# A planner's weights for row maxima, and one broadcast moved down a DMA queue, in an attention kernel

## The chip, the cores and the metric

The kernel runs on one core of a Trainium2 chip. The metric is the device time of one execution in microseconds (us), the median of several. TensorE does the matmuls, VectorE, ScalarE and GpSimd work on tiles beside it, SyncE (SP) issues the DMAs. The profile calls the first four PE, DVE, ACT and POOL; PEld is TensorE's loading of weights.

## What is computed

The input x has 2 batches of 2048 tokens by 512 features, all in fp32. After a layer norm, `xn` goes two ways:

```python
q, k, v = (xn @ W for W in (Wq, Wk, Wv))            # 16 heads of 32
scores  = einsum('bthd,bshd->bhts', q, k) * tril    # masked scores become 0, not -inf
attn    = softmax(scores / 2048**0.5)
s       = einsum('bhts,bshd->bthd', attn, v) @ Wo
g       = silu(layernorm(xn)*gamma+beta @ ternary(weight).T + bias)
out     = x + s * g
```

A masked score is multiplied by zero and so still takes part in the softmax, as exp(0).

## The kernel before, in words

**Three stages.** The first (to about 397 us) makes queries, keys, values and the gate, chunk by chunk of 512 tokens, and stores them to HBM. The second, from about 397 to 1412 us, is attention in 8 *quads*, each of four heads of one batch. The third, the tail, multiplies by Wo in 8 chunks of 512 tokens, 0 to 3 of batch 0 and 4 to 7 of batch 1, multiplies with the gate and adds x.

**Steps of a quad.** A quad has 40 steps (`STEPS`, L31), numbered 0 to 39 here. A step (c, j) takes query chunk c (512 wide) and key tile j (128 rows); the last four steps of each c lie on the diagonal and are 512, 384, 256 and 128 wide. `GROUPS` (L36) takes steps two by two. In a step, for each of the four heads:

- `scores` (L1465) makes the scores two steps *ahead*, one matmul of up to 512 columns, into one of three PSUM banks psS; ScalarE's `exps` (L1053) turns them into weights in Pb.
- `max_scores` (L1359) makes what the planner puts at this step of *row maxima*: scores with queries on the partitions, 512 columns to a PSUM bank psM, of which there are three. VectorE takes the maximum of each bank (L1173 for plain banks, L1170 for banks that end on the diagonal and are masked). TensorE waits for the bank three entries back before it fills it again.
- then comes the step's *section*: `values` (L1488) adds weights times values into psO, all four heads side by side in 8 short matmuls. At steps for which `by_tensor` (L111) holds, 8 more (L1495) add up the weights into psL: the *row sums*. At the other steps GpSimd adds the weights (L914) or, at j = 0, the tile itself is the start of the sum.

`by_tensor` holds in a quad at steps 2, 6, 8, 10, 16, 18, 20, 22, 28, 30, 32, 34, 36, 38 (in the last quad at more). At j = 0 of a chunk, `row_sums` (L1504) follows the section with four times two matmuls from GpSimd's sums, so that section is as long as one with row sums.

**The order on TensorE** is written out in `quad` (L1519 to L1540): the scores and maxima of step s (`ahead(s)`), then the section of s; on a diagonal `ahead(s)`, `ahead(s + 1)`, then both sections.

**The planner.** A quad has 140 banks of maxima (`max_banks`), sorted by the query chunk that they belong to, and four *turns* (transposes of finished maxima, L1349). The maxima of a chunk of queries must be there before its first scores. `UPFRONT` banks of a quad are made in steps 19 to 39 of the quad before, the rest in its own steps 0 to 18; quad 0 makes 102 of its own there. `step_room` (L135) gives each step a weight: the time of its scores, and a `section` term. `max_entries` (L189) goes along (step, head) and hands out the next entries while the cost given out so far is behind the weight passed so far. The result is the *share* of each step and head (`SHARES`), read by TensorE, ScalarE and VectorE alike.

**The tail's DMAs** are all issued by SP in one order (`chunk`, L818). For chunk n: for n < 4, wait for `al_done` of chunk n and request the numerators `ac` of chunk n + 4 (L752); wait for the chunk's outputs (L828) and store them (L829); for n < 4 request x and gate of chunk n + 4 (`xr`, `gr`, L755, L756). Each is 1 MB. The sums of the softmax of batch 1 are inverted on VectorE (L1241). `spread(1)` (L740), at n = 1, waits for them, puts them to HBM (L743, 32 KB), waits until they have landed (L744), waits for the last products of batch 0 (L745) and issues 16 requests that read them back, each broadcast over 32 partitions (L748, `rb`). Only chunk 7 needs `rb`: GpSimd multiplies its numerators by it (L958). For each other chunk of batch 1 the numerators come already divided.

For chunk n ScalarE makes `ah` (L1061) from `ac`, VectorE `al`, the rest of it (L1258), then TensorE 32 matmuls with `ah` (L1565) and 16 with `al` (L1555); VectorE multiplies by the gate (L1295, `sg`) and adds x (L1297, `oo`), each in four pieces. VectorE makes `al` of chunk n + 1 before the outputs of chunk n. Outputs of chunk n wait for the store of chunk n - 2 to land.

Of the kernel before, what the change touches and what calls it, by code (L numbers as in the profile page):

```python
# [13 lines left out]
P = 128  # L14
B, T, D, H = 2, 2048, 512, 16
# [5 lines left out]
CW = 512  # L21
# [62 lines left out]
def width(s):  # L84
    c, j = STEPS[s]
    return CW - max(0, j - CT * c) * P
# [15 lines left out]
def by_gpsimd(s, last):  # L102


    c, j = STEPS[s]
    if last and c > 0 and (on_diagonal(s) or (c, j) in [(3, 7), (3, 11)]):
        return False
    return j % 2 == 1 or not last and (c, j) in EXTRA


def by_tensor(s, last):  # L111
    return STEPS[s][1] > 0 and not by_gpsimd(s, last)
# [22 lines left out]
def step_room(s):  # L135


    c, j = STEPS[s]
    ahead = STEPS[(s + 2) % NSTEP]
    scores = 1.1 + 4.4 * (CW - max(0, ahead[1] - CT * ahead[0]) * P) / CW  # L140
    section = 1.5 * width(s) / CW
    return scores / 2.5 + section - (1 if j == 0 else 0)


# [28 lines left out]
NX = 4  # L173
# [93 lines left out]
def build(nc, x, Wq, Wk, Wv, Wo, Wf, bias, gamma, beta, out):  # L267
    top = ExitStack()
    with top:
        def sem(name):  # L270
            return top.enter_context(nc.semaphore(name))

        def sbuf(stack, name, shape, dt):
            return stack.enter_context(nc.sbuf_tensor(name, shape, dt))
# [17 lines left out]
        r_rows = nc.dram_tensor("r_rows", [B * H, CW], F32).ap()  # L292
# [67 lines left out]
        lr = sbuf(pc, "lr", [P, H * CW // P], F32)  # L360
# [118 lines left out]
        lrec_done = sem("lrec_done")  # L479
        r_out = sem("r_out")  # L480
# [59 lines left out]
        def numerators(b, c):  # L540
            return num_t[bass.ds(b * D, D), c * CW:(c + 1) * CW].rearrange("(k p) w -> p k w", p=P)
# [43 lines left out]
        def _(sp):  # L585
# [116 lines left out]
            def store_last(qn):  # L702

                c, cols = NCH - 1, slice((NCH - 1) * CW, NCH * CW)
                sp.wait_ge(ost_done, START + qn * NCH + c + 1).then_inc(sp_waited, 1)
                sp.dma_start(num_t[bass.ds(qn * P, P), cols], cum[c % 2][:]).then_inc(ost_out[c % 2], 16)
                sp.wait_ge(lst_done, START + qn * NCH + c + 1).then_inc(sp_waited, 1)
                sp.dma_start(l_rows[bass.ds(qn * HQ, HQ), :], E[c % 2][::DH, :]).then_inc(lst_out, 16)

            def divisors(qn, c):  # L710


                i = c % 2
                sp.wait_ge(lst_done, START + qn * NCH + c + 1).then_inc(sp_waited, 1)
                for h in range(HQ):
                    sp.dma_start(lc[h * DH:(h + 1) * DH, :], E[i][h * DH:h * DH + 1, :]).then_inc(lc_in, 16)  # L716
# [20 lines left out]
            def denominators(b):  # L737
                sp.dma_start(lr[:], l_rows[bass.ds(b * H, H), :].rearrange("r (a w) -> (r a) w", w=H * CW // P)).then_inc(lr_in, 16)

            def spread(b):  # L740

                sp.wait_ge(lrec_done, b + 1)
                sp.dma_start(r_rows[bass.ds(b * H, H), :].rearrange("r (a w) -> (r a) w", w=H * CW // P), lr[:]).then_inc(r_out, 16)  # L743
                sp.wait_ge(r_out, (b + 1) * 16)  # L744
                sp.wait_ge(mul_done, START + b * KT)  # L745
                for k in range(KT):
                    for h in range(HQ):
                        sp.dma_start(rb[h * DH:(h + 1) * DH, k, :],  # L748
                                     r_rows[bass.ds(b * H + k * HQ + h, 1), :].broadcast_to([DH, CW])).then_inc(r_in, 16)

            def load_numerators(b, c):
                sp.dma_start(ac[c][:], numerators(b, c)).then_inc(ac_in[c], 16)  # L752
# [5 lines left out]
            def quad(qn, par, more, follows):  # L758
                if follows:
                    store_last(qn - 1)  # L760
                    load_chunk(qn, 1)
                    sp.wait_ge(pv_done, START + qn * NSTEP)
                if not more:

                    sp.wait_ge(lst_out, START + NQ * 16)
                    denominators(0)
                    sp.dma_start(wo_s[:], w_o).then_inc(wo_in, 16)

                if follows:
                    store_maxima(qn, 2)  # L770
                divisors(qn, 0)
                back(qn, 0)
                if not follows:
                    store_maxima(qn, 2)
                store_divided(qn, 0)
                load_chunk(qn, 2)
                if more:

                    load_half(qn + 1, 1 - par, 1)
                else:  # L780
                    for i in range(2):
                        sp.wait_ge(ost_out[i], START + NQ * NCH // 2 * 16)
                    load_numerators(0, 0)
                    load_numerators(0, 1)
                divisors(qn, 1)
                store_maxima(qn, 3)
                back(qn, 1)
                if more:
                    load_values(qn + 1, 1 - par)
                    store_maxima(qn + 1, 0)  # L790
                else:
                    load_numerators(0, 2)
                    sp.wait_ge(pv_done, START + qn * NSTEP + STEPS.index((2, 0)))
                    load_xg(0)
                divisors(qn, 2)
                store_divided(qn, 1)
                load_chunk(qn, 3)
                back(qn, 2)
                store_divided(qn, 2)
                if more:  # L800
                    load_chunk(qn + 1, 0)
                    store_maxima(qn + 1, 1)
                else:
                    spread(0)
                    sp.wait_ge(wo_done, 2)
                    load_numerators(0, NDIV)
                if qn + 2 < NQUAD:

                    sp.wait_ge(pv_done, START + qn * NSTEP + STEPS.index((NCH - 1, NT // 2)))
                    load_half(qn + 2, par, 0)  # L810
            quads(quad)
            store_last(NQUAD - 1)
            attention_over(sp)
# [3 lines left out]

            def chunk(n, b, c):  # L818
                if n == 1:
                    spread(1)  # L820
                if n + NX < NCHUNK:

                    sp.wait_ge(al_done, START + (n + 1) * KT)
                    load_numerators(1, c)

                parts = [slice(j, j + 1) for j in range(CT)] if n + 1 == NCHUNK else [slice(0, CT)]
                for part in parts:
                    sp.wait_ge(oo_done, START + n * CT + part.stop)  # L828
                    sp.dma_start(out_v[n][:, part], oo[c % 2][:, part]).then_inc(oo_out[c % 2], 16)  # L829
                if n + NX < NCHUNK:  # L830
                    load_xg(n + NX)
# [767 lines left out]
```

## Time and profile before

| | |
|---|---|
| three timed runs | 1515.99 us median (1511.0 to 1517.45) |
| the profiled execution | 1510.48 us, its span 1508.8 us |
| granted TensorE clock, mean | 0.995 |
| busy: TensorE / VectorE / ScalarE / GpSimd | 1474.0 / 1045.3 / 772.3 / 922.6 us |
| HBM | 201 MB moved, 133 GB/s mean |

The span is the time from the first to the last instruction of the program; the profiled execution's own time is 1.7 us longer. In a timeline a row gives start, duration, engine, line, operation, and how many like it were merged; in square brackets stands the idle time before it and who ended it. TensorE's matmuls overlap, so their pace is read from the distance of their starts.

### The profile page before, as it was taken

Reading aid. Unit: us, or ns where it says so; the run is one execution under the profiler, and the core shown is the slowest. Engines: PE = TensorE matmul, PEld = TensorE weight load, DVE = VectorE, ACT = ScalarE, POOL = GpSimd, SP = SyncE. Lnnn points to the kernel's source line nnn. Section 1 sums busy time; section 2 is a strip of 40 time slices with the busy share of each in tenths; the row PEclk is TensorE's granted clock in tenths of the full one; section 3 lists DMA queues with packets and bytes.
Section 4 is the critical chain, followed back from the end, with each engine's and each line's share of the span. In section 5 each row is a group of like instructions: output and inputs, shape, how many; then the busy total and the mean of one; then the engine's idle time right before and its main releaser. Section 6 shows DMA issues by size and latency. Waiting matters only on the chain.

```text
span 1508.8 us, 24424 instructions
## 1 busy us (share of the span) xinstructions
PE 1474.0 (98%) x8458; PEld 898.5 (60%) x8458; DVE 1045.3 (69%) x2413; ACT 772.3 (51%) x1615; POOL 922.6 (61%) x747
## 2 busy tenths in 40 slices
PE   6999999999999999999999999999999999999998
PEld 5888888888544455555555545555554554554686
DVE  7546566554688777777777777777777777773557
ACT  4333223332455666666566665666665666657311
POOL 4100000000477989888998998989998898867401
PEclk9999999999999999999999999999999999999999
DMA  6668965557834425242451533525145152123687
GB/s 206 183 179 235 264 182 170 159 161 202 229 86 109 104 54 113 84 108 54 104 127 30 136 88 74 112 68 122 44 109 134 30 112 81 51 85 128 229 291 297
DMA packets 118395, 201.25 MB, mean 133 GB/s; under 512 B 23264, under 2 KB 40800, under 8 KB 117248
## 3 DMA queue, kind: packets, MB, share of 16 engines
q1 hardware_dynamic: 118272, 199.69, 48.2%
q8 instruction: 67, 1.10, 0.3%
q14 instruction: 56, 0.46, 0.1%
HBM read 123.02 MB, written 76.09 MB: 132 GB/s over the span
## 4 chain that ended last, share of the span: by engine, by line
PE 83%; DVE 8%; DMA 4%; SPq 2%; ACT 2%; issue 1%; POOL 0%; ACTq 0%; DVEq 0%; POOLq 0%
PE psP L1384 21%; PE psS L1465 17%; PE psO L1488 17%; PE psM L1359 16%; PE psL L1495 6%; DVE mx L1173 3%; DVE psM L1170 2%; PE psT L1309 2%; PE psL L1504 2%; DMA out<-oo 1%; ACT acc L1053 1%; PE psD L1565 1%; DMA lc<-E 1%; SPq L716 1%; DMA r_rows<-lr 1%
## 5 line engine op out<-in xcount | busy, mean ns | idle before, releaser
L1053 ACT ACTIVATE Pb<-psS 128x512 f32<-128x512 f32 (+3 forms) x1215 | 563.6, 539 | 361.2 <-PE psS L1465 356.9
L1173 DVE TENSOR_REDUCE mx<-psM 128x1 f32<-128x512 f32 x768 | 484.7, 683 | 136.1 <-PE psM L1359 134.7
L914 POOL TENSOR_TENSOR acc<-acc,Pb 128x1024 f32<-128x1024 f32 (+2 forms) x284 | 543.5, 1943 | 39.9 <-ACT Pb L1053 31.8
L1465 PE MATMUL psS<-half 97*128 97x512 f32 (+1 forms) x1247 | 473.9, 397 | 2.1 <-ACT Pb L1053 0.9
L1359 PE MATMUL psM<-half 96*128 96x512 f32 (+3 forms) x1280 | 458.8, 384 | 10.8 <-DVE mx L1173 4.4
L1465 PEld LDWEIGHTS psS<-half 97*128 97x128 f32 x1247 | 234.8, 190 | 239.4 <-ACT Pb L1053 104.1
L1488 PE MATMUL psO<-Pb,Vs 128*32 128x512 f32 (+3 forms) x2496 | 290.5, 537 | 0.0
L1359 PEld LDWEIGHTS psM<-half 96*128 96x128 f32 x1280 | 236.2, 191 | 83.1 <-DVE mx L1173 32.9
L1170 DVE CUSTOM_DVE_ANT_0 psM<-psM,negm 128x256 f32<-128x256 f32 (+3 forms) x512 | 238.3, 518 | 59.0 <-PE psM L1359 58.5
L914 POOL TENSOR_TENSOR acc<-Pb 128x1024 f32<-128x1024 f32 x48 | 113.4, 2382 | 25.9 <-ACT Pb L1053 25.8
L1190 DVE TENSOR_TENSOR st_lo<-psP,st_hi 128x512 fp32r<-128x512 f32 x64 | 43.9, 688 | 118.0 <-ACT st_hi L1008 118.0
L892 POOL TENSOR_SCALAR_AFFINE_SELECT Pb<-Pb 128x256 f32<-128x256 f32 x240 | 94.0, 407 | 50.9 <-ACT Pb L1053 47.8
L1488 PEld LDWEIGHTS psO<-Pb,Vs 128*32 128x32 f32 x2496 | 56.0, 109 | 94.5 <-issue 44.4
L1495 PE MATMUL psL<-Pb,ones 128*32 128x512 f32 (+3 forms) x976 | 110.9, 526 | 0.0
L852 POOL TENSOR_TENSOR rstd<-ve,mhalf 128x4 f32<-128x4 f32 x8 | 8.1, 1009 | 160.9 <-DVE ve L1106 160.8
L1008 ACT CAST st_hi<-psP 128x512 fp32r<-128x512 f32 x64 | 37.2, 587 | 107.5 <-PE psP L1384 107.4
L1384 PE MATMUL psP<-xh,w_hi 128*128 128x512 f32 x256 | 73.4, 409 | 0.8 <-ACT xh L971 0.8
L1170 DVE DVE_READ_ACCUMULATOR2_ANT mx<- 128x1 f32 x512 | 72.4, 141 | 0.0
L852 POOL TENSOR_TENSOR r<-ve,mhalf 128x4 f32<-128x4 f32 x8 | 8.1, 1009 | 103.7 <-DVE ve L1120 103.7
L1384 PE MATMUL psP<-xl,w_hi 128*128 128x512 f32 x256 | 70.9, 399 | 0.0
L1384 PE MATMUL psP<-xh,w_lo 128*128 128x512 f32 x256 | 70.0, 395 | 0.0
L1495 PEld LDWEIGHTS psL<-Pb,ones 128*32 128x32 f32 x976 | 31.7, 110 | 56.8 <-issue 51.4
(104 smaller groups left out, 1466.3 us busy)
## 6 DMA issues: line engine op xcount, KB each, us to landing
half<-q_hi SPq DMA_DIRECT2D x32, 512.0 KB, 10.0
half<-k_hi SPq DMA_DIRECT2D x32, 512.0 KB, 10.1
q_hi<-st_hi SPq DMA_DIRECT2D x32, 256.0 KB, 4.5
q_lo<-st_lo SPq DMA_DIRECT2D x32, 256.0 KB, 4.9
gate<-gs SPq DMA_DIRECT2D x32, 256.0 KB, 2.2
k_hi<-st_hi SPq DMA_DIRECT2D x32, 256.0 KB, 2.8
k_lo<-st_lo SPq DMA_DIRECT2D x32, 256.0 KB, 3.0
v_quad<-vs SPq DMA_DIRECT2D x32, 256.0 KB, 3.3
```

Of the source, the lines that this page charges most:

```text
L892: g.affine_select(out=tile, in_=tile, compare_op=ALU.is_ge, fill=0.0, base=0, pattern=[[0, 2], [1, P]], channel_multiplier=-1).then_inc(se ...
L914: g.tensor_tensor(to[:, :, o:], one, Pb[s % RING][:, heads, o:], ALU.add).then_inc(sum_done, 1)
L1008: a.copy(st_hi[k % 4][:], psP[k % 4][:]).then_inc(hi_done, 1)
L1053: a.activation(weights(s, h)[:, o:], score_bank(s * HQ + h, last)[:, o:], ACT.Exp, scale=SCALE).then_inc(exp_done, 1)
L1170: ins = v.tensor_tensor_reduce(out=part, in0=part, in1=negm[:, CW - w:], scale=1.0, scalar=-3e38, op0=ALU.add, op1=ALU.max, accum_out=flat ...
L1173: ins = v.tensor_reduce(flat[:, heads, slots], bank[:, 0:ns * w].rearrange("p (a b c) -> p a b c", a=nh, c=w), AX.X, ALU.max)
L1190: v.tensor_tensor(st_lo[k % 4][:], psP[k % 4][:], st_hi[k % 4][:].bitcast(F32), ALU.subtract).then_inc(lo_done, 1)
L1359: ins = t.matmul(bank[:, z * w:(z + 1) * w], Q[tile // HALF][0:STACK, h, tile % HALF * P:(tile % HALF + 1) * P], K[half][0:STACK, h, k0 - ...
L1384: ins = t.matmul(psP[bank][:], left(k), right(k), start=(a + k == 0), stop=(a == len(parts) - 1 and k == KT - 1))
L1465: t.matmul(score_bank(n, last)[:, o:], Ks[par][j // HALF][0:MROW + 1, h, j % HALF * P:(j % HALF + 1) * P], Qs[par][c // 2][0:MROW + 1, h, ...
L1488: ins = t.matmul(psO[hc, o:], V[:, j, hc], weights(s, h)[:, o:], start=(j == 0), stop=(s == last_step[c]), skip_group_check=True)
L1495: ins = t.matmul(psL[h * DH:(h + 1) * DH, o:], ones[:, 0:DH], weights(s, h)[:, o:], start=first, stop=False, skip_group_check=True)
```

## The change

It has two parts. The weight of a step's section in the planner is no longer 1.5 for every step, but 2 where the step takes row sums on TensorE and 1 elsewhere, times the step's width. The entries and their order stay the same; where they are made changes, and `UPFRONT` goes from 75 to 76. The number of entries (banks and turns) at steps 0 to 39, worked out from the code:

```text
quad 0 before  3 4 6 5 5 7 6 7 5 3 5 5 4 7 6 6 6 6 7 4 | 3 3 4 3 3 5 4 4 4 5 4 5 4 4 4 4 3 3 3 2
quad 0 after   3 3 6 5 5 6 9 6 6 3 6 4 4 5 6 5 8 5 8 4 | 3 3 4 4 2 4 4 4 4 5 5 4 5 4 5 3 4 2 4 2
quads 1-6 bef. 2 3 3 4 3 4 4 3 4 2 3 3 3 4 4 4 4 4 5 4 | 3 3 4 3 3 5 4 4 4 5 4 5 4 4 4 4 3 3 3 2
quads 1-6 aft. 2 2 4 3 3 3 5 3 4 2 4 3 2 4 4 3 5 3 6 4 | 3 3 4 4 2 4 4 4 4 5 5 4 5 4 5 3 4 2 4 2
```

Share 30 holds a turn among its entries before and after. In share 18 of quads 1 to 6 all banks lie on the diagonal: one of two 256-wide pieces and four of 384 before, two and four after; the bank that is added comes out of share 17.

The second part takes the put of the reciprocals and the broadcast apart. For batch 1 the put stays at n = 1 and no longer waits for its landing there; the wait and the 16 requests come at n = 3, behind the request for chunk 7's numerators. For batch 0 both stay where they were, one behind the other.

```diff
@@ step_room
-    section = 1.5 * width(s) / CW
+    section = (2 if by_tensor(s, False) else 1) * width(s) / CW
     return scores / 2.5 + section - (1 if j == 0 else 0)
@@ sync engine
-            def spread(b):
-
+            def put_reciprocals(b):
                 sp.wait_ge(lrec_done, b + 1)
                 sp.dma_start(r_rows[bass.ds(b * H, H), :].rearrange("r (a w) -> (r a) w", w=H * CW // P), lr[:]).then_inc(r_out, 16)
+
+            def spread(b):
+
                 sp.wait_ge(r_out, (b + 1) * 16)
                 sp.wait_ge(mul_done, START + b * KT)
@@ quad
                 else:
+                    put_reciprocals(0)
                     spread(0)
@@ chunk
                 if n == 1:
-                    spread(1)
+                    put_reciprocals(1)
                 if n + NX < NCHUNK:
 
                     sp.wait_ge(al_done, START + (n + 1) * KT)
                     load_numerators(1, c)
+                if n == NX - 1:
+
+                    spread(1)
```

## Rows read from the trace of the kernel before

**Rows 1.** The page: busy us (share of the span) and instructions of each engine.
```profile
PE 1474.0 (98%) x8458; PEld 898.5 (60%) x8458; DVE 1045.3 (69%) x2413; ACT 772.3 (51%) x1615; POOL 922.6 (61%) x747
```
**Rows 2.** Stretches: length, busy PE, PEld, DVE, ACT, POOL, clock, DMA share, GB/s.
```profile
409.20:475.11 65.91, 63.11 (x331) 30.71 (x330) 54.70 (x133) 33.42 (x66) 44.49 (x34) 0.97 0.53 109
796.40:923.00 126.60, 125.47 (x792) 65.42 (x791) 96.61 (x246) 78.36 (x172) 113.38 (x92) 1.00 0.38 91
```
**Rows 3.** Waits for VectorE in those two stretches: us, times, longest.
```profile
PEld psM L1359 <- DVE mx L1173: 12.5, 38, 0.4
...
PEld psM L1359 <- DVE mx L1173: 2.8, 8, 0.9
```
**Rows 4.** TensorE's timeline, quad 3: steps 13 to 14, 17 to 18, 24 to 25, 32 to 33.
```profile
834.00 1.07 PE L1488 MATMUL psO<-Pb,Vs 128*32 128x512 f32 x8
...
835.34 0.40 PE L1359 MATMUL psM<-half 96*128 96x512 f32 x1
...
836.75 0.40 PE L1359 MATMUL psM<-half 96*128 96x512 f32 x1
837.08 1.06 PE L1488 MATMUL psO<-Pb,Vs 128*32 128x512 f32 x8
...
847.36 1.07 PE L1488 MATMUL psO<-Pb,Vs 128*32 128x512 f32 x8
850.95 1.07 PE L1488 MATMUL psO<-Pb,Vs 128*32 128x512 f32 x8
...
868.53 1.07 PE L1488 MATMUL psO<-Pb,Vs 128*32 128x512 f32 x8
...
872.93 0.64 PE L1488 MATMUL psO<-Pb,Vs 128*32 128x512 f32 x4
...
897.92 1.06 PE L1488 MATMUL psO<-Pb,Vs 128*32 128x512 f32 x8
...
901.85 1.07 PE L1488 MATMUL psO<-Pb,Vs 128*32 128x512 f32 x8
```
**Rows 5.** Quad 0, sections 15 and 16 on TensorE, and VectorE's six banks between them.
```profile
456.66 1.07 PE L1488 MATMUL psO<-Pb,Vs 128*32 128x512 f32 x8
...
460.80 1.06 PE L1488 MATMUL psO<-Pb,Vs 128*32 128x512 f32 x8
...
458.44 3.68 DVE L1173 TENSOR_REDUCE mx<-psM 128x1 f32<-128x512 f32 x6 [0.45 <-PE psM L1359]
```
**Rows 6.** SP's timeline in the tail.
```profile
1434.62 1.13 SPq L743 DMA_DIRECT2D r_rows<-lr  x1
1446.46 7.49 SPq L748 DMA_DIRECT2D rb<-r_rows  x16
...
1471.58 2.47 SPq L829 DMA_DIRECT2D out<-oo  x1
```
**Rows 7.** Two stretches of the tail, columns as in rows 2.
```profile
1443.00:1456.00 13.00, 13.00 (x59) 10.78 (x58) 7.05 (x12) 2.19 (x4) 0.00 (x0) 1.00 0.44 125
1456.00:1490.00 34.00, 34.00 (x152) 28.09 (x150) 19.97 (x31) 6.86 (x12) 5.48 (x4) 1.00 1.04 386
```
**Rows 8.** Timelines of TensorE, VectorE and GpSimd in the tail.
```profile
1412.03 0.50 PE L1565 MATMUL psD<-wo_h,ah 128*128 128x512 f32 x1
...
1488.32 0.39 PE L1565 MATMUL psD<-wo_h,ah 128*128 128x512 f32 x1
...
1493.84 1.86 PE L1555 MATMUL psD<-wo_h,al 128*128 128x512 f32 x4 [3.55 <-DVE al L1258]
...
1503.75 1.07 PE L1555 MATMUL psD<-wo_h,al 128*128 128x512 f32 x4
...
1485.27 0.69 DVE L1295 TENSOR_TENSOR sg<-psD,gr 128x512 f32<-128x512 f32 x1 [2.72 <-issue]
...
1491.30 2.49 DVE L1258 TENSOR_TENSOR al<-ac,ah 128x512 fp32r<-128x512 f32 x4
...
1482.69 5.48 POOL L958 TENSOR_TENSOR ac<-ac,rb 128x512 f32<-128x512 f32 x4 [69.24 <-DMA ac<-num_t]
```

## Prediction, made before the change was built

> **What bounds the kernel now.** I read the page first. TensorE is busy for 1474.0 us, 98% of the span [rows 1]. A busy TensorE is not yet one at its pace, so I next read stretches: in one middle quad (q3) TensorE is busy 125.47 of 126.60 us and VectorE 96.61, while in the first half of quad 0 VectorE has 54.70 us of work in 65.91 us [rows 2]. The waits say what that means. In that half quad 0 TensorE's weight loads for maxima wait 12.5 us in 38 places for VectorE's plain maxima, in the whole of quad 3 only 2.8 us in 8 [rows 3]. So the middle quads run at TensorE's own pace with a few waits, and the start of quad 0 at VectorE's.
>
> The timeline of single steps gives the two paces. I call an interval the time from one step's section (its psO run, and the psL run where it takes row sums) to the next step's. It holds that section, and then four scores and the *next* step's share of maxima. With four banks an interval takes 837.08 - 834.00 = 3.08 us after a section without row sums and 901.85 - 897.92 = 3.93 us after one with them [rows 4]. Scores and banks alternate there, (836.75 - 835.34)/6 = 0.235 us apart [rows 4]. That is TensorE's price of one more bank. VectorE takes 3.68/6 = 0.61 us for a bank, and with six banks the interval grew to 460.80 - 456.66 = 4.14 us [rows 5].
>
> The tail (from 1412.03) is TensorE's too, 10.88 us a chunk, until 1488.32. Chunk 7 then starts, but its first low-part product comes at 1493.84, after an idle 3.55 us, released by VectorE's al [rows 8]. The way back in the timelines: VectorE makes al for chunk 7 only at 1491.30, behind chunk 5's outputs, which began late, at 1485.27, after an idle 2.72 us [rows 8]. They waited for chunk 3's store, which SP issued at 1471.58, 13.7 us before [rows 6, 8]. SP itself was late: it put the reciprocals at 1434.62 and stood until they had landed, 11.8 us later at 1446.46, then issued 16 spreading requests (7.49 us), so the request for chunk 5's numerators went out only after 1453.95 [rows 6]. Between 1443 and 1456 the DMA engines were at 0.44 of their time, against 1.04 behind it [rows 7].
>
> **Part 1, the shares of maxima.** No instruction is added or removed; the same entries run in the same order. From the code (the diff section has the counts), 11 of some 143 entries of a middle quad change step: shares of steps with row sums grow, the others shrink. TensorE's own work of a quad is conserved, so only waits can change.
>
> What matters is the order in the code: share s stands *ahead* of section s. A larger share at a row-sum step therefore mostly follows a section *without* row sums (steps alternate), and the long section comes only after it. The three psM banks tie them: the last bank of a share of k is issued only when VectorE has done k-3. From [rows 5]: VectorE starts 458.44 - 456.66 = 1.78 us after the section's start, needs 0.61 a bank, and the rest up to the next section is 4.14 - 1.78 - 3 x 0.61 = 0.53. So the interval cannot be shorter than 1.78 + 0.61(k-3) + 0.53: 2.92 for four banks (TensorE's 3.08 decides), 3.53 for five, against TensorE's 3.08 + 0.235 = 3.32. **Five banks after a short section cost a wait of 0.2 us.** After a long section both are 0.85 longer: five banks took 872.93 - 868.53 = 4.40 us, against 3.93 + 0.235 = 4.17, again 0.23 of wait [rows 4].
>
> Middle quad, by interval: shares 6, 16, 32 and 34 go from four banks to five after a short section: +0.8. Share 30 goes to five entries, one a turn: +0.2, taken as the others. Share 18 goes from five entries of small diagonal banks to six; its interval is 850.95 - 847.36 = 3.59 us now [rows 4], and its bound rises to about 4.2 by one more bank of two 256-wide pieces (0.77 us of VectorE), of which 0.24 is TensorE's own: +0.4, less 0.15 in the interval before it, which loses that bank. Shares 25 and 31 go from five to four after a long section: -0.23 each. Sum: 0.8 + 0.2 + 0.25 - 0.46 = +0.8; I take +0.6, since a wait taken in one interval can save one in the next. Six quads: +3.6. Quad 7 has only its own half: +0.6. Quad 0's first half is at VectorE's pace nearly throughout, and there each bank costs 0.61 in whichever interval it stands: 0, between -3 (eight moved entries, each saving 0.61 - 0.235 = 0.37) and +2. Its second half: +0.2. Together **+4.4 us**, bounds -5 (quad 0's -3 and 0.3 in each other quad, a tenth of the 2.8 us of [rows 3]) and +11 (0.3 a moved bank in every quad).
>
> The row gives VectorE 0.61 us from one maximum's start to the next [rows 5]. The Trainium skill ("VectorE: DVE Perf Modes", the section on the TRN2 errata) prices a 512-wide read of PSUM at 120 + 512 cycles of 0.96 GHz, 0.66 us; by that a share of five after a short section would cost 0.1 us more, one taken away after a long section would save 0.1 more, and this part would come to about +7. No sum here uses it; the measured rate is the faster one.
>
> **Part 2, the reciprocals.** `put_reciprocals(1)` stays at chunk 1, the 16 requests move behind the request for chunk 7's numerators. SP goes on at 1434.62 + 1.13 = 1435.8 instead of 1453.95 [rows 6]. It then meets only the full queues: with 1 MB per request at 386 GB/s [rows 7], a request is served every 2.7 us. In order: ac5, out1, xr5, gr5, ac6, out2, xr6, gr6, ac7 (served by 1467), 16 spreads (7.49 us of issuing, about 3 of transfer), out3 served by 1473, xr7, gr7, out4 by 1481. Every DMA that the move passes is counted here: out3 now stands behind the 16 spreads, and still lands some 10 us before the 1485.27 at which VectorE had it. The put has 11.8 us to land and is asked for some 24 us later: no wait.
>
> Against these stand the dates that TensorE sets at 10.88 a chunk. Chunk 5's outputs on VectorE can start when its first product is ready, about 1474.7, and out3 lands at about that time; they end at 1480.1, al for chunk 7 at 1482.6, with 5.7 us to spare, its ah (GpSimd's products 5.48 us after the spreads land near 1471, then ScalarE) by 1480. TensorE reaches chunk 7 at 1488.32 as before and does not stop: it ends at 1488.32 + 10.88 = 1499.2, against 1503.75 + 1.07 = 1504.8 [rows 8]. That takes in the slower matmuls after the idle time, 0.43 apart at 1495.50 and 0.23 at 1488.32 [rows 8]. **-5.6 us.** Bounds: 0 if another wait takes the place, -6 (nothing beyond TensorE's pace is to be had).
>
> **Sum.** 4.4 - 5.6 = -1.2 us against the profiled execution's 1510.48 us (span 1508.8), so 1509.3. That execution is below all three timed runs (median 1515.99, 1511.0 to 1517.45), so for the median: **1514.8 us**.
>
> **Rivals.** *The maxima find room.* If VectorE's backlog, not the next section, is what an interval pays for, each moved entry saves 0.37 wherever VectorE sets the pace: 8 in quad 0 and, in each of 6.6 quads, 3 (17, 25, 31), without the new waits: 28 x 0.37 = -10.4, with the tail -16: 1500. For it: the 12.5 us of waits in quad 0 [rows 3]. Against it: the order in the code, by which the long section comes after the larger share. Chance 0.13.
>
> *VectorE becomes the pace of the middle quads (the other side).* It decides if VectorE is still busy when a share of five begins, because a diagonal bank with its read-out or a row reduction of psO and psL stands in front; then the full 4.14 - 3.08 = 1.06 for two banks is paid, 0.53 for one, and the share of six at step 18 brings the row maxima of the fourth chunk late as well. Then each of the six larger shares costs 0.4 more: 2.4 + 0.6 = 3.0 a quad, over 6.6 quads +20, less the tail's 5.6: 1530. It decides from 2.0 us a quad on, where the sum leaves what can be told from none. For it: 18 is already the worst stretch. Against it: 30 us of VectorE idle in a middle quad [rows 2]. Chance 0.08.
>
> *The tail gains nothing*, if DMA engines at 1.04 with 386 GB/s are the limit [rows 7] and the empty stretch was slack: +4.4, 1520. Against it: the empty 13 us are followed by a wait that TensorE pays. Chance 0.05. That the plan doesn't move anything is ruled out by working the shares out from the code.
>
> **How the numbers follow.** Forecast 0.74, rivals as above. A difference under about 0.5% (7.6 us) can't be told from none. Faster by more takes the first rival and a rest, 0.14; slower the second and a rest, 0.09; same 0.77. Range: the bounds -5 to +11 and -6 to 0 put the sum between -11 and +11; cut at one in ten on each side and with the runs' own spread, 1505 to 1522.
>
> **What would show it.** Right: the intervals that hold shares 6, 16, 32 and 34 at 3.5 us instead of 3.08; those with 25 and 31 at 3.9 instead of 4.40; a middle quad of 127.2 instead of 126.6 us; r_rows at 1435 and no SP gap behind it; DMA share near 1.0 from 1443 to 1456; TensorE without idle time in the tail and no slow matmuls at its end. Wrong: a middle quad under 126 or over 129, a half quad 0 under 63, or VectorE still waiting for a store at chunk 5.

## The result and the profile after

| | before | changed |
|---|---|---|
| median of 20 executions | 1512.9 us (1507.97 to 1519.61) | 1518.03 us (1516.55 to 1521.53) |
| the profiled execution, its span | 1510.48, 1508.8 us | 1517.22, 1515.5 us |
| middle quad 3 | 126.6 us | 127.9 us |
| the tail, from its first product (1412.03, 1424.2) to VectorE's last output | 94.2 us | 88.8 us |

The ratio is 1.003, 95% interval 1.002 to 1.0039: the changed kernel is 5.1 us slower, where the sum had said 1.2 us faster. 1518.03 us lies in the stated range and the difference is within 0.5%, but the sign of the sum was wrong. The forecast of 1514.8 us also started from a median of three runs, 1515.99 us, that was 3.1 us above the one of twenty.

The page of the changed kernel, busy time of each engine, against [rows 1]:

```profile
PE 1479.3 (98%) x8458; PEld 891.5 (59%) x8458; DVE 1045.1 (69%) x2413; ACT 779.5 (51%) x1615; POOL 922.8 (61%) x747
```

The counts are the same and VectorE's work is too. The page alone says nothing more, so I went to the same stretches as before. TensorE's and VectorE's lines stand 6 further down in the changed kernel (L1173 is L1179 there). The changed kernel's quad 3 and three stretches of its tail, columns as in [rows 2]:

```profile
798.80:926.60 127.80, 126.33 (x789) 64.86 (x788) 96.55 (x244) 79.28 (x173) 113.41 (x92) 1.00 0.38 90
1427.00:1455.00 28.00, 28.00 (x126) 23.17 (x125) 18.16 (x29) 4.37 (x8) 0.18 (x1) 1.00 0.98 355
1455.00:1468.00 13.00, 13.00 (x59) 10.78 (x58) 9.72 (x16) 2.19 (x4) 0.00 (x0) 1.00 1.05 398
1468.00:1500.00 32.00, 32.00 (x143) 26.51 (x142) 22.40 (x34) 6.86 (x12) 5.49 (x4) 1.00 0.97 342
```

A middle quad is 1.3 us longer at a granted clock of 1.00 (1.26 to 1.32 in quads 1 to 4 and 6), and VectorE's busy time in it is unchanged. In the tail TensorE now never stops, and the DMA engines have lost their empty stretch (0.44 in [rows 7], 0.98 to 1.05 now).

**Where the quad's time went.** The waits of the changed kernel's quad 3 for VectorE:

```profile
PEld psM L1365 <- DVE mx L1179: 6.2, 18, 0.8
PEld psM L1365 <- DVE mx L1176: 3.2, 9, 0.5
```

[rows 3] had 2.8 us in 8 places for the plain maxima, and the masked ones were at:

```profile
PEld psM L1359 <- DVE mx L1170: 2.5, 8, 0.5
```

TensorE's timeline gives the places (sections 5 and 6, 15 and 16, 17 and 18, 21 and 22, 24 and 25):

```profile
812.38 1.06 PE L1494 MATMUL psO<-Pb,Vs 128*32 128x512 f32 x8
815.98 1.06 PE L1494 MATMUL psO<-Pb,Vs 128*32 128x512 f32 x8
...
842.70 1.06 PE L1494 MATMUL psO<-Pb,Vs 128*32 128x512 f32 x8
846.24 1.06 PE L1494 MATMUL psO<-Pb,Vs 128*32 128x512 f32 x8
850.14 1.06 PE L1494 MATMUL psO<-Pb,Vs 128*32 128x512 f32 x8
854.49 1.06 PE L1494 MATMUL psO<-Pb,Vs 128*32 128x512 f32 x8
...
864.38 0.83 PE L1494 MATMUL psO<-Pb,Vs 128*32 128x384 f32 x8
869.70 0.64 PE L1494 MATMUL psO<-Pb,Vs 128*32 128x256 f32 x8
...
872.59 1.07 PE L1494 MATMUL psO<-Pb,Vs 128*32 128x512 f32 x8
876.51 1.06 PE L1494 MATMUL psO<-Pb,Vs 128*32 128x512 f32 x8
```

The pair 21 and 22 is not in the rows ahead of the prediction; in the kernel before it took 4.55 us:

```profile
860.85 0.83 PE L1488 MATMUL psO<-Pb,Vs 128*32 128x384 f32 x8
865.40 0.64 PE L1488 MATMUL psO<-Pb,Vs 128*32 128x256 f32 x8
```

I read every interval of quad 3 in this way. Named by the share that it holds (a pair of steps on a diagonal has its two shares in one interval), these moved. TensorE's own part of a difference is 0.235 for each entry more or less; what is beyond it is the wait, and the sum was a sum of waits:

| share | before | changed | difference | beyond TensorE's own | in the sum |
|---|---|---|---|---|---|
| 6, 16, 32, 34 (four to five) | 3.06 to 3.08 | 3.54 to 3.60 | +1.96 | +1.02 | +0.8 |
| 30 (a turn as the fifth) | 2.94 | 3.55 | +0.62 | +0.38 | +0.2 |
| 18 (six, diagonal), with 17 (one less) | 3.59, 4.13 | 4.35, 3.90 | +0.76, -0.24 | +0.52 | +0.25 |
| 22 with 23 (seven to eight) | 4.55 | 5.32 | +0.77 | +0.53 | none |
| 25, 31 (five to four, long section) | 4.41, 4.40 | 3.93, 3.93 | -0.95 | -0.48 | -0.46 |
| 0 with 1 (five to four) | 3.21 | 2.66 | -0.55 | -0.32 | none |
| 10 with 11, 38 with 39 (one more each) | 4.63, 4.47 | 4.63, 4.47 | 0 | -0.47 | none |
| 27, 28 (same number) | 3.84, 3.47 | 3.74, 3.30 | -0.26 | -0.26 | none |
| 2 with 3 (same number), 15 (one less) | 4.80, 3.06 | 5.03, 2.92 | +0.23, -0.14 | +0.33 | none |
| the others together | | | | about 0 | none |

The column beyond TensorE's own makes +1.3, the quad's own difference; the last one makes the prediction's +0.8.

**The tail.** SP's timeline of the changed kernel:

```profile
1446.88 1.14 SPq L742 DMA_DIRECT2D r_rows<-lr  x1
1448.06 2.58 SPq L754 DMA_DIRECT2D ac<-num_t  x1
...
1467.13 4.60 SPq L754 DMA_DIRECT2D ac<-num_t  x1
1471.84 9.57 SPq L750 DMA_DIRECT2D rb<-r_rows  x16
1481.46 0.42 SPq L835 DMA_DIRECT2D out<-oo  x1
```

The put is followed at once by the request that used to stand behind its landing, 11.8 us, and behind the 16 spreads [rows 6]. The spreads now come after the request for chunk 7's numerators. What VectorE, GpSimd and TensorE make of it, in three fences:

```profile
1490.31 0.69 DVE L1301 TENSOR_TENSOR sg<-psD,gr 128x512 f32<-128x512 f32 x1 [6.15 <-DMA out<-oo]
...
1496.88 2.49 DVE L1264 TENSOR_TENSOR al<-ac,ah 128x512 fp32r<-128x512 f32 x4
```

```profile
1488.27 5.49 POOL L964 TENSOR_TENSOR ac<-ac,rb 128x512 f32<-128x512 f32 x4 [61.09 <-DMA rb<-r_rows]
```

```profile
1500.53 0.39 PE L1571 MATMUL psD<-wo_h,ah 128*128 128x512 f32 x1
...
1510.50 1.07 PE L1561 MATMUL psD<-wo_h,al 128*128 128x512 f32 x4
```

The tail begins 12.2 us later than in [rows 8], as the quads ahead of it are longer (3 us of it are a fall of the clock in quad 5, told in the last section), and with the 5.4 us that it gives back that makes the 6.7 us between the two spans. VectorE still waits for the store of chunk 3 (6.15 us), but it makes al for chunk 7 from 1496.88 to 1499.37, and TensorE comes to chunk 7 at 1500.53: the wait is covered. Chunk 7 runs to 1510.50 + 1.07 = 1511.57, 11.04 us without a stop; [rows 8] had an idle 3.55 us in it and slow matmuls behind, where the granted clock was 0.57 from 1494 to 1498.

### The profile page after: what moved, and what is told of

Its sections match the earlier page's. It is cut to its first block, busy times and chain, and to the rows that moved or that the text cites. A ratio compares the mean times of both kernels' runs of the same rounds, so it can differ in the third digit from the quotient of the medians.

```text
span 1515.5 us, 24424 instructions
## 1 busy us (share of the span) xinstructions
PE 1479.3 (98%) x8458; PEld 891.5 (59%) x8458; DVE 1045.1 (69%) x2413; ACT 779.5 (51%) x1615; POOL 922.8 (61%) x747
## 4 chain that ended last, share of the span: by engine, by line
PE 84%; DVE 9%; DMA 3%; SPq 1%; ACT 1%; issue 1%; POOL 0%; ACTq 0%; DVEq 0%; POOLq 0%
PE psP L1390 19%; PE psO L1494 17%; PE psS L1471 16%; PE psM L1365 16%; PE psL L1501 6%; DVE mx L1179 4%; PE psD L1571 4%; DVE psM L1176 3%; PE psD L1561 2%; PE psT L1315 2%; PE psL L1510 2%; DMA half<-k_lo 1%; DMA lc<-E 1%; SPq L716 1%; PE psM L1471 1%
## 5 line engine op out<-in xcount | busy, mean ns | idle before, releaser
L1059 ACT ACTIVATE Pb<-psS 128x512 f32<-128x512 f32 (+3 forms) x1215 | 570.7, 536 | 369.8 <-PE psS L1471 356.5
L1179 DVE TENSOR_REDUCE mx<-psM 128x1 f32<-128x512 f32 x768 | 482.6, 683 | 144.6 <-PE psM L1365 144.6
```

Source lines behind the costliest of these rows:

```text
L1059: a.activation(weights(s, h)[:, o:], score_bank(s * HQ + h, last)[:, o:], ACT.Exp, scale=SCALE).then_inc(exp_done, 1)
L1179: ins = v.tensor_reduce(flat[:, heads, slots], bank[:, 0:ns * w].rearrange("p (a b c) -> p a b c", a=nh, c=w), AX.X, ALU.max)
```

## The experiments

Their times are medians; each ratio is against the kernel before on the same chip (1512.3 to 1512.8 us). "Theory A" in the expectations is the one of the prediction, worked out with what the changed kernel's trace had shown.

### Each part alone

```diff
 tail_only: the changed kernel with
-    section = (2 if by_tensor(s, False) else 1) * width(s) / CW
+    section = 1.5 * width(s) / CW
 plan_only: the changed kernel with
-                put_reciprocals(0) / put_reciprocals(1) / the later spread(1)
+                spread(0) and spread(1) with put and wait in one, as before
```

> Part 2 alone (the old weights, 1.5 for every section). Theory A (part 2 does all it was worked out to do, and the loss is the planner's): TensorE without idle time in the tail, the tail 5.4 us shorter as in the changed kernel, the quads at 126.6 us as before; 1512.9 - 5.4 = 1507.5 us. Rival B (the two parts hang together, the tail's gain is only the shift of work behind slower quads): a gain under 2 us.

> Part 1 alone (weights 2 and 1, SP as before). Theory A: middle quads 127.85 us, quad 0 0.9 us longer, together 13 to 14 us less the irregular 3.5 us of one quad, so +10 us: 1523. My own sum on record had +4.4 for this part, its upper bound +11. Rival B (the parts hang together): +5 or less.

Measured: tail_only 1510.53 us, ratio 0.9982 (0.9966 to 0.9998); plan_only 1521.52, ratio 1.0065 (1.0042 to 1.0089). Part 1 costs 8.7 us alone, near the 10 of theory A and twice the 4.4 of the prediction. In tail_only TensorE does not stop in the tail, as theory A had it, but the kernel is 3 us slower than its 1507.5. Part 2 gives 2.3 us alone, and part 1 with part 2 is 5.1 slower, so the two lines of subtraction (2.3 and 3.5) fall short of the 5.4 us that the profiles show in the tail: from the last psO run of quad 7 to the end of the span it takes 92.7 us in tail_only as in the changed kernel, 98.1 before. In the two profiled executions the rest went to places that part 2 does not touch, at a lower granted clock: against the kernel before, tail_only took 4.5 us more in quad 0 and 3.1 us more in quad 5. That the medians hide it in the same places is not shown. Two stretches of tail_only, from the start of quad 0, and one of the kernel before (columns as in [rows 2]):

```profile
394.40:406.00 11.60, 11.46 (x67) 5.79 (x67) 9.08 (x18) 5.67 (x11) 9.71 (x8) 0.92 0.68 211
406.00:480.00 74.00, 71.40 (x357) 34.38 (x355) 58.09 (x148) 36.06 (x74) 45.79 (x38) 0.91 0.47 100
```

```profile
408.00:480.00 72.00, 68.94 (x370) 34.15 (x372) 60.22 (x157) 37.24 (x77) 47.75 (x41) 0.98 0.50 104
```

Quad 0 took 150.8 us in that execution and 146.3 in the one of the kernel before, with the same code in it. Executions of tail_only with a mean clock of 0.996 or 0.997 took 1503.6 to 1507.5 us, those at 0.991 to 0.994 took 1509.1 to 1512.3. The median is of both, and so part 2's value needs a pair in which both sides share everything else (the last experiment).

### The weights the other way round

```diff
 plan_swapped: the kernel before with
-    section = 1.5 * width(s) / CW
+    section = (1 if by_tensor(s, False) else 2) * width(s) / CW
```

> The weights exchanged: 1 where the section takes row sums, 2 elsewhere, so that larger shares come behind the long sections. SP as before. Theory A (VectorE starts on a share only 0.8 us after the section ahead of it has ended, so only the size of a share counts: five entries cost 0.2 us of wait behind a long section as behind a short one): the quads get longer than 126.6 too, about as much as with the changed weights, +0.5 to +1.5 us each, in all +3 to +10. Rival C (the changed weights fail because the larger share stands ahead of the long section and not behind it): the quads get shorter, -0.5 us or more each.

Measured: 1511.14 us, ratio 0.9983 (0.9971 to 0.9994). A middle quad fell by 0.3 us, to 126.2; theory A had it rise by 0.5 to 1.5, rival C fall by 0.5 or more, so both missed. The price of a fifth bank behind a long section, on which theory A rested, can be read by itself. TensorE's timeline of plan_swapped, sections 12 and 13, shows what it costs:

```profile
834.35 1.06 PE L1488 MATMUL psO<-Pb,Vs 128*32 128x512 f32 x8
838.75 1.06 PE L1488 MATMUL psO<-Pb,Vs 128*32 128x512 f32 x8
```

4.40 us with five, 3.92 with four: +0.48, the same as 3.07 to 3.55 after a short section, as theory A had assumed. **Where the fifth bank stands is indifferent**; it costs 0.48 in both. What decides is how many intervals are over the bound, and by how much. The swapped plan adds a bank at about this price at five shares (5, 13, 19, 26 and 33) and one in the pair 0 with 1 (+0.44), and takes entries out of full ones: the interval of share 18 falls by 0.75, the pair 8 with 9 by 0.47, 25 by 0.49, 36 with 37 by 0.49. Shares 27 and 28 hold as many as before, and their intervals fell too, by 0.41 and 0.39, behind a share 25 with one entry less; this fits a wait passed on, but no run separates it.

### A bank of the next share inside a long section

If VectorE is short of work while a long section runs, as the prediction's rival "The maxima find room" supposed, a bank between its two halves should let it start sooner.

```diff
 inside: tail_only, and in section()
             values(...)
+            inside(s)        # the first bank of the next share, taken out of it there
             row sums or sums from GpSimd
```

> Part 2 with the old weights, and in every section that takes row sums the first bank of the next share goes between psO's run and psL's (TensorE's order alone; entries, shares and the other engines' orders stay). Theory A (VectorE stands idle during long sections because its share comes only behind them): quad 0's first half, where VectorE sets the pace, gets 3 to 6 us shorter, the long intervals with five entries fall from 4.40 to about 4.2, a middle quad loses 0.5 to 1 us; in all 8 to 12 us under the version with part 2 alone. Rival D (the waits are a matter of the bank ring, three psM banks, whenever they are filled): no gain over part 2 alone, or a loss from one more change between kinds of matmul in each long section (about 0.1 us each, 14 a quad).

Measured: 1564.23 us, ratio 1.0331 (1.0306 to 1.0355), 134.1 us a middle quad. Both theories missed by far. The timeline of TensorE in inside:

```profile
857.58 1.07 PE L1506 MATMUL psO<-Pb,Vs 128*32 128x512 f32 x8
858.57 0.50 PE L1370 MATMUL psM<-half 96*128 96x512 f32 x1
859.00 1.06 PE L1523 MATMUL psL<-acc,ones 128*32 128x512 f32 x8
860.00 0.72 PE L1476 MATMUL psS<-half 97*128 97x512 f32 x2
```

The bank stands between the start of psO's run at 857.58 and of psL's at 859.00, 1.42 us, where psL's run follows after 0.88 in the changed kernel (872.59 and 873.47): it costs 0.54 there against 0.235 between scores. It is the same, 1.36 to 1.43 us, in all 96 such places behind 500 us, so it is not a wait that comes and goes. The share that lost the bank gives back less than its 0.235: most long intervals off the diagonal grew by about 0.44, where 0.54 - 0.235 would be 0.31. The waits for ScalarE of quad 3 in inside, and of the kernel before:

```profile
PEld psS L1476 <- ACT Pb L1059: 18.7, 41, 0.8
```

```profile
PEld psS L1465 <- ACT Pb L1053: 14.0, 26, 0.8
```

Scores wait for a free psS bank, and so for ScalarE, more often. That a bank of maxima between two scores had been filling this wait is an inference from these lines. 18 intervals of the quad grew, by 0.10 to 0.57 us, each with a long section or a pair of a diagonal, 7.7 us together.

### Fewer banks over the bound

```diff
 level: tail_only, with the shares of quads 1 to 7 written out
+LEVEL = [2,3,3,4,3,4,4,3,3,2,4,3,3,4,4,4,4,4,5, 4,3,3,4,3,4,4,4,4,4,5,4,4,4,4,4,4,3,2,4,3]
+level(SHARES)    # entries of a step = LEVEL[s], in the old order; quad 0 from step 19 on
 recip_later: tail_only, and the row reciprocals of the third query chunk later, GpSimd's division by them too
-RECIPROCALS_AT = {..., STEPS.index((3, 3)): 2}
-DIVIDED_AT = {..., FIRST[3] + 2: 2}
+RECIPROCALS_AT = {..., STEPS.index((3, 5)): 2}
+DIVIDED_AT = {..., FIRST[3] + 3: 2}
 level_recip: both
```

Against the kernel before, the level plan takes one entry out of each of the shares 8, 25, 31 and 37, where the interval is at VectorE's pace, and puts one more into each of 10, 24, 38 and 39.

> Part 2 with a level plan, written out by hand for steps 0 to 39: from the intervals where one more entry cost 0.48 us (shares 25, 31, and the pairs 8 with 9 and 36 with 37) one entry each is taken and put where the three plans so far show room: one to the pair 10 with 11 (4.63 us with six and with seven), two to the pair 38 with 39, one to share 24 (2.24 to 2.40). Quad 0's first half as before. Theory A (an entry costs 0.48 us where the interval is at VectorE's pace, 0.235 or less elsewhere, so that only evenness counts): each middle quad 4 x 0.48 - 0.2 = 1.7 us shorter, 124.9 us, in all -11 and with part 2 -14 to -16: 1497 to 1499. Rival E (a wait taken out comes back in a neighbour): middle quads at 126 or more.

> Part 2 with the old weights, and VectorE's reciprocal of the third chunk's denominators at step 29 instead of 27, GpSimd's division one group later. Theory F (VectorE stands there for the landing of lc, TensorE waits 0.65 us in every quad, and in quad 5, where the landing takes 2.5 to 2.8 us instead of 1.7, long enough for the granted clock to fall for 6.8 us; that took about 3 us of part 2's gain in some executions): interval 26 falls from 3.84 to about 3.1, quad 5 is as long as its neighbours with no low clock in it, and the kernel takes 0.65 x 7 + up to 3 less than part 2 alone, 4 to 7 us: 1503 to 1506. Rival G (the low clock in quad 5 has nothing to do with the wait): it stays, and the gain is at most 4.5.

> Both of the above. Theories A and F together: 1497 - 5 = about 1492 to 1494, middle quads at 124.3 us. If the two take the same waits away (both touch the stretch around shares 25 to 28), 1496.

Measured: level 1500.88 us, ratio 0.9917 (0.9899 to 0.9934); recip_later 1504.09, 0.9941 (0.9922 to 0.9961); level_recip 1500.98, 0.9924 (0.9904 to 0.9943). A run of the level plan in another group (level_again, below) gave 1500.47. Its quad 3, window and waits:

```profile
792.60:918.10 125.50, 124.45 (x790) 65.31 (x789) 95.96 (x245) 77.62 (x172) 113.35 (x92) 1.00 0.38 92
```

```profile
PEld psM L1386 <- DVE mx L1197: 2.4, 8, 0.5
PEld psM L1386 <- DVE mx L1200: 1.6, 4, 0.8
```

The same work in 125.5 us where the kernel before takes 126.6. Shares 25 and 31 give 0.49 and 0.47, the pairs 8 with 9 and 36 with 37 0.40 and 0.42. Where the entries went they cost 0.17 at share 24, 0.20 for the two of the pair 38 with 39, and nothing in the pair 10 with 11, which takes 4.63 us with six or with seven. Four other intervals moved by +0.23 to -0.10 with the same number of entries; in three of them (shares 2, 7, and 20 with 21) the entries stand at other heads of the step than before. Theory A had 124.9 us a quad and 1497 to 1499 us; rival E, 126 or more, falls.

recip_later took 0.76 off one interval of each quad, the one that holds share 27, 3.84 before:

```profile
878.49 1.06 PE L1494 MATMUL psO<-Pb,Vs 128*32 128x512 f32 x8
881.57 1.06 PE L1494 MATMUL psO<-Pb,Vs 128*32 128x512 f32 x8
```

and it kept the clock up in quad 5 (see the last section). Together the two gave no more than the level plan alone, where 1492 to 1496 had been expected. Quad 3 did get shorter, 125.0 us, but quad 1 took 128.7. In its trace TensorE stands there for ScalarE's weights, and ScalarE for a DMA:

```profile
650.36 0.63 ACT L1093 ACTIVATE E<-E 128x512 f32<-128x512 f32 x1 [2.27 <-DMA E<-m_rows]
```

```profile
652.13 0.51 PE L1492 MATMUL psS<-half 97*128 97x512 f32 x1 [2.01 <-ACT Pb L1080]
```

SP requests these maxima only when the store of the divided numerators has landed, and that store waits for the division that recip_later moves back: it was issued at 642.04 us and landed at 646.07. The granted clock was 0.51 from 653 to 656. recip_later's profile has the same wait in quad 1, 1.62 us at the full clock, and 127.7 us for that quad; tail_only's has neither. So the later reciprocal takes a wait away in every quad and makes a new one in quad 1.

### VectorE's half of the price taken away

half_reduce is the changed kernel with VectorE's plain maxima over half of the columns of each bank. It leaves half of the columns out of these maxima, and so computes another result.

```diff
-  ins = v.tensor_reduce(..., bank[...].rearrange(...), ...)
+  ins = v.tensor_reduce(..., bank[...].rearrange(...)[:, :, :, 0:w // 2], ...)
```

> The changed kernel, with VectorE's plain maxima over the first half of each section of columns only (it leaves half of the columns out of the maxima, so a bank costs it about 0.34 us instead of 0.61). Theory A (intervals with five entries are at VectorE's pace through the ring of three banks): those that hold shares 6, 16, 32, 34 fall from 3.54 to TensorE's 3.31 and quad 0's first half, now 79 us from step 0 to 19, falls to about 70; a middle quad 2 to 3 us shorter. Rival H (TensorE's switch between kinds of matmul, or ScalarE's pace on the scores, sets five entries' price): 3.5 stays and middle quads stay over 127.

Measured: 1482.4 us, ratio 0.9799 (0.9777 to 0.9821). Sections 15 and 16, where the changed kernel takes 3.54:

```profile
825.33 1.07 PE L1494 MATMUL psO<-Pb,Vs 128*32 128x512 f32 x8
828.62 1.06 PE L1494 MATMUL psO<-Pb,Vs 128*32 128x512 f32 x8
```

3.29, with 3.31 and 3.29 at shares 32 and 34: this is the 3.08 + 0.235 that the prediction gave as TensorE's own. Rival H falls. So of the 0.48 for a fifth bank half is TensorE's and half is the wait for VectorE. The pair 22 with 23 fell from 5.32 to 4.66, so its excess was VectorE's too. Share 18 did not fall (4.35): its banks are diagonal ones, which this kernel leaves whole. A middle quad took 123.7 us, 4.2 less than the changed kernel's and more than the 2 to 3 expected.

### The four shares that the sum had wrong

```diff
 four_back: the changed kernel, with shares 17, 18, 23 and 24 of every quad as before
+for pair in ((17, 18), (23, 24)):
+    SHARES[...] = OLD[...]
```

> The changed kernel with four shares put back as they were before: 17 and 18, 23 and 24 (two entries a quad). Theory I (what the forecast left out or took too small is in these places: a full bank of small diagonal pieces in front of section 18, and an eighth entry in the pair 22 with 23): the intervals that hold share 18 and shares 22 with 23 fall back from 4.35 and 5.32 to 3.59 and 4.55, those in front and behind rise from 3.90 to 4.13 and from 2.00 to 2.24; a middle quad 127.85 - 1.53 + 0.48 = 126.8 us, the kernel 7 us under the changed one: 1511. Rival J (the loss is spread over all larger shares and the waits only move): a middle quad at 127.4 or more.

Measured: 1509.96 us, ratio 0.9985 (0.9972 to 0.9997), quad 3 126.8 us: against the changed kernel's 1518.03 it is 8 us less. Intervals 17 to 18 and 21 to 22 are back at 3.59 and 4.55, and every other one is as in the changed kernel to 0.02 us. Two of the eleven shares that had grown carry 1.05 of the 1.3 us of a quad.

### The tail beside an equal plan

level_again is level, and level_oldtail is level with part 2 undone.

```diff
 level_oldtail: level with
-                put_reciprocals(1), and spread(1) at n == NX - 1
+                spread(1), with put and wait, at n == 1
```

> The level plan with part 2 once more, beside the next kernel: 1500.9 us again, ratio 0.992.

> The level plan with SP's requests as before the change (no part 2). Theory K (part 2 is worth 5.4 us in every execution): 5.4 us over the level plan with part 2, 1506.3, TensorE idle for 3 to 4 us ahead of the last chunk. Rival L (the timed runs give only half, 2.7 us, as with part 2 alone, because the low clock of the wait in quad 5 or elsewhere eats the rest): 1503.5.

Measured: 1500.47 us, ratio 0.9916 (0.9899 to 0.9933), and 1506.79, 0.9956 (0.9939 to 0.9973). **Part 2 is worth 6.3 us** here. TensorE of level_oldtail at the start of its last chunk:

```profile
1488.25 2.07 PE L1576 MATMUL psD<-wo_h,al 128*128 128x512 f32 x4 [3.46 <-DVE al L1279]
```

It is the idle time of [rows 8] again, 3.46 us for 3.55. From the tail's first product to the end of the span, the profiles of all nine runs with part 2 have 91.3 us, the four without it 95.7 to 97.6 (96.7 in the kernel before, 97.6 here). So part 2 takes away whatever the old order cost in that execution, 4.4 to 6.3 us.

## Why the prediction was wrong in sign, and what in it was right

**Right.** *Part 2.* The mechanism, the order and the size: 5.4 us in the profiled tail, 6.3 between two kernels alike in all else, for the -5.6 and the -6 that was its bound. One date in it was wrong: the spreads were to take 7.49 us of issuing and took 9.57, and out3 was to land at the time VectorE came to it; VectorE waited 6.15 us for it. "VectorE still waiting for a store at chunk 5" had been named as a sign of being wrong, and it came; what it was to stand for, an idle TensorE, did not, as the 5.7 us of slack covered it (al for chunk 7 was done 1.16 us before TensorE came to that chunk). The DMA step "a request is served every 2.7 us" held: issuing took 2.58 us for the request behind the put and 2.0 to 2.9 for the next six.

*The price of a single bank after a short section.* An interval of four after a short section was to go from 3.08 to 3.5 with five: 3.54 to 3.60. The one after a long section was to fall to 3.9: 3.93. TensorE's own floor, 3.32, is what half_reduce shows (3.29 to 3.31). The bound 1.78 + 0.61(k-3) + 0.53 gives 3.53 for five with VectorE's 0.61. By the Trainium skill ("VectorE: DVE Perf Modes", the section on the TRN2 errata) a bank takes 0.66, which would put five banks at 3.63, an estimate with the other two terms as they are; the trace has three of the four at 3.54 or 3.55, nearer to the measured rate, and one at 3.60.

*Quad 0's first half*, not contradicted. Zero was taken, between -3 and +2. The stretch of [rows 2] went from 65.91 to 65.40 us, and steps 0 to 3 took 1.3 us more. But the granted clock was 0.97 in that stretch before and 1.00 in the changed kernel, and it differs from one execution to the next in quad 0, so neither figure shows a gain or a loss.

**Wrong.** The term of the sum that failed is the one for the middle quads, "+0.8; I take +0.6". It measured +1.3 (1.24 in quad 7). By the table of intervals above:

- **The pair 22 with 23, +0.53 that no step had.** On a diagonal two shares are made ahead of two sections. This pair had seven entries and gets an eighth. The step looked at shares one by one ("four banks to five") and priced by that; a pair's interval was not held against a bound.
- **Share 18, +0.52 for +0.25.** The bound, 4.2, was near the interval, 4.35. But "+0.4, less 0.15 in the interval before it" took TensorE's own 0.24 off in the 0.4 and then took the same bank's leaving share 17 off once more (that interval gave back TensorE's 0.24 and no more); the rest is the bound's 0.15.
- **Five entries after a short section, +1.40 for +1.0.** A wait of 0.2 was worked out for each; it is 0.25 for the banks and 0.38 where the fifth entry is a turn ("taken as the others").
- **What came back, -0.65 for the -0.2 of the discount.** That "a wait taken in one interval can save one in the next" is borne out by shares 27 and 28 (-0.26). The pair 0 with 1 gave back 0.32 beyond TensorE's own, and two pairs took an entry for nothing. Against these, share 15 gave 0.14 instead of 0.235, and the pair 2 with 3 took 0.23 more with as many entries as before. None of it had been worked out, so the 0.6 was a guess on top of a list with two holes.

In place of 0.6, six quads took 1.3 each and quad 7 took 1.24, which is +4.8, and quad 0 took 0.9 us for the 0.2 that it was given, so the sum becomes -1.2 + 4.8 + 0.7 = +4.3, against the measured +5.1. With the sum's bounds of -11 and +11 a median inside the range says little for it. four_back takes the first two items out, and the quad falls to 126.8.

The rivals. *The maxima find room* fell: what leaves VectorE's intervals does save 0.4 to 0.5 us (shares 25 and 31 here, four places in the level plan), but the change puts seven entries into such intervals, or over the edge of them (6, 16, 18, 30, 32, 34, the pair 22 with 23), and takes three out (25, 31, the pair 0 with 1). *VectorE becomes the pace* is right about share 18 and the pair 22 with 23, where VectorE takes diagonal banks first, but not in the other five of its six larger shares; 1.3 us a quad is below the 2.0 from which it was said to decide. *The tail gains nothing* falls. What was argued from the order in the code, that the larger share stands after a short section, carried no weight: plan_swapped shows that a fifth entry costs 0.48 either way. The sum was right to charge the waits; it was wrong to charge them for single shares alone, instead of holding every interval, the pairs too, against its bound.

Of the kernels that compute the whole result, those with the level plan were the fastest: 1500.5 to 1500.9 us, some 12 us under the kernel before and 17 under the changed one, with part 2 in it (level_recip, 1500.98, is no different).

## What to carry to other kernels

The price of one more item in a stretch is a step function: here 0.235 us while TensorE sets the pace, 0.48 (0.76 and 0.77 at two places where VectorE takes diagonal banks first) from the point where VectorE does, and a stretch already past that point is the one from which to take; read each stretch's length against that bound before weighting it. A broadcast that only the last consumer needs belongs behind the requests for which others wait, with its put issued early and its wait late. A matmul costs less between others of its own kind (0.235 us here) than between runs of another kind (0.54).

## What the runs showed of the hardware

**The clock falls in the middle of the attention, behind some waits of TensorE of 1.3 to 2 us and not behind others.** In quad 5 of the changed kernel and of tail_only, VectorE's reciprocals of the row sums come late, and TensorE stands. In the changed kernel, first VectorE and then TensorE:

```profile
1138.80 0.25 DVE L1273 RECIPROCAL lc<-lc 128x16 f32<-128x16 f32 x1 [2.28 <-DMA lc<-E]
```

```profile
1139.65 0.49 PE L1365 MATMUL psM<-half 96*128 96x512 f32 x1 [1.49 <-DVE mx L1179]
...
1145.00 1.94 PE L1494 MATMUL psO<-Pb,Vs 128*32 128x512 f32 x8
```

The changed kernel's windows around it:

```profile
1137.00:1139.00 2.00, 1.16 (x5) 0.60 (x4) 0.20 (x2) 1.95 (x4) 2.00 (x2) 1.00 0.36 131
1141.00:1143.00 2.00, 2.00 (x11) 1.64 (x8) 1.15 (x3) 1.05 (x2) 2.00 (x2) 0.58 0.76 217
1143.00:1145.00 2.00, 2.00 (x8) 1.58 (x7) 1.70 (x11) 1.06 (x3) 1.55 (x1) 0.50 0.09 23
```

The granted clock is 1.00 during the wait, and falls to 0.50 (1.2 GHz) within 2 us of its end, when TensorE is busy again; a psO run then lasts 1.94 us instead of 1.06. Intervals 27 to 28 and 28 to 29 took 4.93 and 5.74 us instead of 3.30 and 4.20: 3 us for a wait of 1.49. The profiles of tail_only, four_back and level have the same fall there, behind waits of 1.41, 1.27 and 1.28 us. Behind 1.30 us in the kernel before, 1.34 in plan_only and 1.45 in level_oldtail the clock stayed up, and in level_again, the same kernel as level, it stayed up behind 1.10. So neither the plan nor the length of the wait decides it, and what does is open; the 6.7 us between the two spans hold about 3 us of it. The only other fall in quads 1 to 6 of the thirteen profiles is the one of level_recip, behind 2.01 us, told above. In quad 0 the clock also falls with no wait of 0.6 us or more just ahead of it, as at 425.75 us in the kernel before, to 0.50. In recip_later, where the reciprocals come two steps later, that interval is 3.08 in quad 5 too and the clock stays up, which may be a part of its 6.4 us under tail_only. Why the landing of lc takes 2.8 us in quad 5 and about 1.7 elsewhere was not settled.

**A change of the kind of matmul costs about 0.3 us.** A bank of maxima, with 128 columns of weights, between two runs with 32 (inside) cost 0.54 us, against 0.235 where it alternates with scores, which have 128 too. That is for the change there and back, and whether it is the width or something else in which the two kinds differ was not tried.

**Requests slow down in a full queue.** The 16 broadcasts of 64 KB took 7.49 to 7.52 us to issue in the four runs without part 2, where SP had stood for the landing of the put and the queues had run empty, and 9.32 to 9.83 in the nine with it, behind 1 MB requests.
